# Attention block on one core: ring copies ahead of the store of the denominators, and four smaller moves

## What is computed

```
h = _layernorm(x, ln1_g, ln1_b)
x = _attention(h, h, sa_wq, sa_wk, sa_wv, sa_wo, sa_bo) + x
h = _layernorm(x, ln2_g, ln2_b)
x = _attention(h, cond_emb, ca_wq, ca_wk, ca_wv, ca_wo, ca_bo) + x
h = _layernorm(x, ln3_g, ln3_b)
p = h @ ff_w1 + ff_b1
a, gate = (p[..., :D_FF], p[..., D_FF:])
h = a * jax.nn.gelu(gate, approximate=False) @ ff_w2 + ff_b2
return h + x
```

## Time and profile before

| | us |
|---|---|
| median of three runs | 1690.47 |
| lowest and highest | 1689.78, 1691.63 |
| profiled execution, its time | 1689.77 |
| profiled execution, its span | 1687.9 |
| PE busy | 1676.3 |
| DVE busy | 1396.7 |
| ACT busy | 1249.1 |
| POOL busy | 1082.0 |

### The profile page before, as it was taken

One profiled execution on the slowest core, in us unless ns is written; L12 is line 12 of the kernel. 1 busy time (PEld: TensorE's weight loads), 2 busy tenths in 40 slices (PEclk: granted clock), 3 DMA queues, 4 the chain that ended last, 5 costly groups with the idle time before them and its releaser, 6 DMA issues.

```text
span 1687.9 us, 39061 instructions
## 1 busy us (share of the span) xinstructions
PE 1676.3 (99%) x11712; PEld 1560.7 (92%) x11712; DVE 1396.7 (83%) x2964; ACT 1249.1 (74%) x3378; POOL 1082.0 (64%) x1804
## 2 busy tenths in 40 slices
PE   8999999999999999999999999999999999999999
PEld 8999999999999999999999999999999998888888
DVE  7888788888888888888888888888888987656665
ACT  7788788888888888888888888888888886232221
POOL 7776577777766667687777777777777564231111
PEclk9999999999999999999999999999999999999999
DMA  7776677777776667887787878787776776112110
GB/s 209 187 181 161 171 197 198 205 202 212 198 181 158 158 166 201 233 221 181 192 211 188 210 198 209 195 207 187 191 188 173 196 209 169 51 50 76 62 39 26
DMA packets 301137, 288.91 MB, mean 171 GB/s; under 512 B 103424, under 2 KB 252032, under 8 KB 300928
## 3 DMA queue, kind: packets, MB, share of 16 engines
q1 hardware_dynamic: 246848, 272.76, 61.9%
q10 hardware_dynamic: 54080, 13.65, 3.6%
HBM read 82.98 MB, written 37.49 MB: 71 GB/s over the span
## 4 chain that ended last, share of the span: by engine, by line
PE 96%; DVE 1%; DMA 1%; SPq 0%; issue 0%; ACT 0%; ACTq 0%; DVEq 0%
PE QKB L564 17%; PE PVB L648 14%; PE PTB L577 13%; PE WOP L630 11%; PE VB L499 9%; PE S L466 7%; PE S L467 7%; PE S L1330 5%; PE PTB L1330 5%; PE QKB L546 3%; PE QKB L1352 3%; PE VB L1352 3%; PE QKB L1295 0%; DMA XR<-in_x_dram 0%; DMA HF<-rows 0%
## 5 line engine op out<-in xcount | busy, mean ns | idle before, releaser
L791 ACT ACTIVATE PT<-S,NM 128x256 f32<-128x256 f32 x1024 | 471.9, 473 | 139.2 <-DVE NM L995 138.5
L897 DVE TENSOR_TENSOR PL<-PTB,PH 128x512 fp32r<-128x512 f32 x512 | 350.8, 686 | 123.8 <-ACT PH L819 122.3
L1189 POOL TENSOR_TENSOR ON<-ON,RB 128x256 f32<-128x256 f32 x256 | 188.5, 736 | 272.2 <-DVE ON L1014 247.8
L995 DVE TENSOR_REDUCE NM<-S 128x2 f32<-128x512 f32 x512 | 327.4, 681 | 1.2 <-PE S L467 1.1
L819 ACT ACTIVATE PH<-PTB 128x1024 fp32r<-128x1024 f32 x256 | 264.0, 1031 | 72.0 <-PE PTB L577 71.1
L577 PE MATMUL PTB<-IDN,PT 128*128 128x128 f32 x2048 | 265.5, 272 | 0.6 <-DVE PL L897 0.5
L466 PE MATMUL S<-RX 128*128 128x256 f32 x1012 | 254.0, 283 | 2.1 <-DMA RX<-QKS 2.1
L467 PE MATMUL S<-RX 128*128 128x256 f32 x1012 | 253.7, 283 | 0.0
L564 PE MATMUL QKB<-HT,WQ 128*128 128x512 f32 x936 | 242.0, 394 | 0.2
L630 PEld LDWEIGHTS WOP<-WO,OT 128*128 128x128 f32 x1536 | 217.5, 190 | 19.7
L577 PEld LDWEIGHTS PTB<-IDN,PT 128*128 128x128 f32 x2048 | 229.6, 140 | 1.3 <-DVE PL L897 0.8
(11 more groups left out here) (162 smaller groups left out, 2921.8 us busy)
## 6 DMA issues: line engine op xcount, KB each, us to landing
RX<-QKS SPq DMA_DIRECT2D x506, 192.0 KB, 2.9
RX<-QKS SPq DMA_DIRECT2D x506, 128.0 KB, 2.8
RB<-denominators SPq DMA_DIRECT2D x512, 64.0 KB, 2.7
out_dram<-XR SPq DMA_DIRECT2D x32, 256.0 KB, 3.4
weights_qk<-SPL SPq DMA_DIRECT2D x32, 256.0 KB, 3.4
WQ<-weights_qk SPq DMA_DIRECT2D x32, 256.0 KB, 3.3
rows<-XN SPq DMA_DIRECT2D x23, 256.0 KB, 2.7
rows<-HF SPq DMA_DIRECT2D x22, 256.0 KB, 2.7
```

Source lines behind the costliest of these rows:

```text
L791: last = e.activation(PT[:, c % 2, j * S:(j + 1) * S], S1[:, i, qt * S:(qt + 1) * S], ACT.Exp, bias=NM[:, j:j + 1], accum_out=DEN[:, c % 2 ...
L897: e.tensor_tensor(PL[:, cols], PTB[:, i, :], PH[:, s % 2, cols].bitcast(F32), ALU.subtract).then_inc(a.dve_pl, 1)
L995: e.tensor_reduce(NM[:, i * TT:(i + 1) * TT], S1[:, i, :].rearrange("p (t s) -> p t s", t=TT), AX.X, ALU.max, negate=True).then_inc(a.dve_ ...
```

## The change

SP: from slot 8 on (`PAIRS <= c`) the four ring copies stand ahead of the store of the denominators; in slots 1 to 7 the store stays ahead. The last two quarters of WQ for the feed-forward part are loaded from ACT's queue (`act_load_last`), one chunk at the end of each slot from 248 to 255. PE: behind the last slot the gates of unit 5 stand ahead of the second product of unit 1. In the first slots: DVE normalizes both tiles of sequence 1 in slot 1 instead of one in slot 0 and one in slot 1; the second low part of P of pair 1 is made in slot 2 rather than slot 3; ACT and POOL split weight piece 11 in slot 3 rather than slot 2; POOL splits three pieces of WO at the end of slot 1 and the fourth at the start of slot 2, rather than two in each.

```diff
@@ dve_slot
             if c == 0:
                 dve_weights(e, 5)
-                e.wait_ge(a.pe_h, 2)
-                dve_normalize(e, sl, a, 1, (near(1),), (0,))
-                dve_split_qk(e, 2)
...
-            if c > 2 and sl.has(c - 2) and c < ATT - 1:
+            if c > 3 and sl.has(c - 2) and c < ATT - 1:
                 dve_p_low(e, c - 2, 1)
...
                 e.tensor_copy(VF[:, v // 2 % 2, v % 2, :], VB[:, 0:S]).then_inc(a.dve_vf, 1)
+            if c == 0:
+                dve_split_qk(e, 2)
             if c == 1:
-                dve_normalize(e, sl, a, 1, (near(1),), (1,))
+                e.wait_ge(a.pe_h, 2)
+                dve_normalize(e, sl, a, 1, (near(1),))
...
-                if c == 1 or c >= ATT - 2:
+                if c in (1, 2) or c >= ATT - 2:
                     dve_p_low(e, c - 1, 1)
@@ pool_weights, pool_slot
-            if 1 <= c <= 2:
-                pool_split_wo(e, 0, 0, 2 * c - 2)
-                pool_split_wo(e, 0, 0, 2 * c - 1)
+            if c == 1:
+                pool_split_wo(e, 0, 0, 0)
+                pool_split_wo(e, 0, 0, 1)
+                pool_split_wo(e, 0, 0, 2)
...
+            if c == 2:
+                pool_split_wo(e, 0, 0, 3)
@@ act_attention_slot
+        def act_load_last(e, c):
+
+            quarter, chunk = divmod(c - LAST, 4)
+            if 0 <= quarter < 2:
+                if chunk == 0:
+                    for done in d_ws:
+                        e.wait_ge(done, 16 * QTR * NCH)
+                    e.wait_ge(a.pe_qk, nth_alone(ATT - QUAD + 2 * quarter + 1) + 1)
+                    e.wait_ge(d_wq[quarter], 16 * 4 * (QTR // 2 + 1))
+                e.dma_start(WQ[:, 2 + quarter, chunk, :, :].bitcast(F32), WSQ[1, :, 2 + quarter, chunk, :, :]) \
+                    .then_inc(d_wq[quarter], 16)
+
         def act_attention_slot(e, sl):
             act_slot(e, sl)
-            if -AHEAD <= sl.c < 3:
-                act_weights(e, *((4,), (5,), (6, 7), (8,), (9, 10), (11,))[sl.c + AHEAD])
+            act_load_last(e, sl.c)
+            if -AHEAD <= sl.c < 2 or sl.c == 3:
+                act_weights(e, *((4,), (5,), (6, 7), (8,), (9, 10), (), (11,))[sl.c + AHEAD])
@@ pool_attention_slot
-            if 0 <= sl.c < 3:
-                pool_low(e, *((8,), (10,), (11,))[sl.c])
+            if 0 <= sl.c < 2 or sl.c == 3:
+                pool_low(e, (8, 10, 10, 11)[sl.c])
@@ block.sync
-                if 1 <= c <= ATT:
+                if 1 <= c < PAIRS:
                     save_den(c - 1)
                 if 0 <= c - 1 + AHEAD < ATT and c - 1 >= -AHEAD:
                     k = c - 1 + AHEAD
                     if k >= DIRECT:
                         copy_ring(e, k)
+                if PAIRS <= c <= ATT:
+                    save_den(c - 1)
@@ block.tensor
             pe_second(e, 0)
-            pe_second(e, 1)
             pe_outputs(e, ATT - 2)
             pe_gates(e, EARLY + 1)
+            pe_second(e, 1)
             pe_second(e, 2)
```

More of the change, by code:

```diff
@@ L1711, in fill_weights @@
                 for phase, first in ((0, SLOTS), (1, ATT)):
[L1712 to L1721, removed]
+                    for quarter in range(QTR - 2 * phase):
+                        j = first - 2 * PAIRS + 4 * quarter + 3
+                        freed = nth_joint(j) + 1
                         for chunk in range(4):
-                            if c == at + turns[chunk]:
+                            if c == j - LEAD + 2 + chunk:
                                 if chunk == 0:
@@ L1727, in fill_weights @@
                                     if quarter > 1:
-                                        e.wait_ge(d_wq[quarter % 2], 16 * 4 * (QTR // 2 * phase + quarter // 2))
+                                        e.wait_ge(d_wq[quarter % 2], 16 * 4)
                                 load_quarter(phase, quarter, chunk)
```

## The result

| | before | after |
|---|---|---|
| median, us | 1690.12 | 1947.87 |
| lowest and highest, us | 1688.44, 1691.63 | 1947.42, 1951.58 |
| span of the profiled execution, us | 1687.9 | 1949.8 |

Four runs of each give a ratio of 1.1532, 95% interval 1.1518 to 1.1545: the change costs 258 us. The prediction was 1876 us in a range of 1770 to 1990, so the direction and the range held, and the time came out 72 us above the sum.

A forecast was written before the change was run, and what follows sets the result against it. PE, busy 1676.3 of 1687.9 us, bounds the kernel before; after the change SP's 6.19 us cycle exceeds PE's 5.48. Sum: 1689.8 + 189 - 2.2 - 0.5 - 0.5 = 1876 us, range 1770 to 1990 for 8 in 10.

The forecast's parts named there:

- Part 1: SP's queue from slot 8: the read waits for the denominators' store issued behind the ring copies, so SP sets pace; +189 us.
- L = 2.4: Time in us from the issue of the denominators' store on SP to its landing, in its new place behind four ring copies.
- rival B: The store's flight is that of a loaded machine, 3.25 us in every slot: 2084 us; chance of above 2.9 us: 0.1.
- The cycle around L: SP's slot outside the store's flight: reads 1.20, four ring copies 2.53, satisfied waits 0.06, together 3.79 us; with the flight 6.19.
- Row stores: In 30 slots a store of normalized rows stands between reads and ring on SP, 0.66 us each, not hidden: 20 us.
- The lead of SP: SP's ring copies at first run ahead of PE's need, which takes 4.5 us off the loss.
- Part 2: PE after the last slot: unit 5's gates ahead of unit 1's second product remove a stall, -2.2 us.
- Part 3: Eight last 256 KB refills move from SP's to ScalarE's queue, one a slot from slot 248: 0 to -1 us.
- Part 4: Moves in the first slots remove PE waits of 0.6 and 0.5 us: -0.5 us, between -1.1 and +1.
- A: The store's flight is under 1.69 us, so SP keeps PE's pace and the gains stay: 1686 us; chance 0.05.
- C: Pauses of PE, some 0.7 us in each slot, bring its clock down; chance 0.02.
- D: Something other than SP, VectorE behind its wait for the store, makes the cycle longer than SP's own; chance 0.03.

The follow-up runs named there:

- half-swapped kernel: The changed kernel with the new order of ring copies and store only from slot 128 on, store first in slots 1 to 127: 1836.45 us, ratio 1.0870.

## Why the prediction was right in its mechanism and 72 us short

**Part 1, the mechanism: right.** The loss is the swap's (1.1537 alone, 0.9985 without it), it goes when the read doesn't wait (0.9994), and it doesn't go when VectorE doesn't (1.1578). "SP's waits for the landing should number about 245 and sum to some 400 us": 250 and 367.9.

**L = 2.4: right.** Over the 212 slots from 8 to 251 in which no rows are stored, read off SP's timeline after, the time from the store's issue to the next read is 2.39 in the mean and 2.34 in the median. That was the value of the first of the three places in the earlier trace rows, and the 3.25 of the second, rival B's, is rare: the longest here is 3.57.

**The cycle around L: mis-sized.** In the same 212 slots the reads to the ring take 1.31 and the ring to the store 2.72, together 4.03 where 3.79 was set down (with L, 6.41 instead of 6.19). An ordinary slot takes 1.23 + 2.64 in the median, 0.08 more than was set down. The rest, the larger part, is in single issues: one that takes 0.6 as a rule now and then takes 0.9 to 2.0. One such slot, whose pair of reads takes 2.30 where the next slot's takes 1.13, so that 7.43 us lie between them:

```profile
92.44 2.30 SPq L1661 DMA_DIRECT2D RB<-denominators  x2
...
99.87 1.13 SPq L1661 DMA_DIRECT2D RB<-denominators  x2
```

45 of the 212 slots are over 6.6 us. The kernel before has nearly as many slow issues (46 single ones over 0.9 us or pairs of reads over 1.5, against 51 here), but there SP had slack to absorb them, and the rows chosen for the sum were undisturbed ones; a queue with no slack pays each. 212 x 0.22 = 47 us.

**Row stores: mis-sized.** 20 us were set down for 30 of them, 0.66 each. There are 32 in these slots, and a slot with one takes 7.60 in the mean: 1.19 more than the others: 0.64 for the issue, 0.20 in the ring's issues and 0.33 in L, which is 2.72 there, by rounded means. 32 x (7.60 - 6.19 - 0.66) = 24 us. The two terms give 71 us, which is what the stretch took beyond the forecast: 1602.5 against 245 x 6.19 + 20 - 4.5 = 1532 us. The lead of SP at the start was not read off by itself. The few us that are left of the difference are the 3.1 us of slots 253 to 255 and the gain of Part 2, of which next to nothing shows in the changed kernel.

**The Trainium skill's rule on completion.** The floor that the prediction worked out from the Trainium skill (DMA: Bandwidth & Descriptors, Queues, rings and completion order), a completion that lands only behind the earlier writes of its engine, was 2.15 us for L, with +128 us for the change. The measured 2.34 to 2.39 lies above the floor and the loss is twice that sum, so as a floor for the usual slot it holds (it was reckoned from a median landing; the shortest single L is 1.99). That the copies ahead set L isn't shown: L doesn't grow from two to four of them (2.39, 2.40, 2.36 where SP stood idle ahead of the read).

**Part 2: right about the stall, half wrong about the gain.** What the step left out is that with the outputs POOL's next work comes earlier too. "Nothing else is late" was read from durations that VectorE only has while POOL rests. In the changed kernel itself, PE waits 0.28 and 0.54 us at the change-over, and from slot 255 to the end only 0.1 us is gained.

The Trainium skill (SBUF — State Buffer, Who interferes with whom) has a rule for this: VectorE instructions with two SBUF inputs, or in a mode that uses both of its ports, contend with GpSimd for a port pair, and the second to come waits. The rows above agree in that both engines' instructions get longer (0.43 to 0.85, 0.69 to 1.11, and 2.82 to 4.35 for four); they don't show which instruction blocked which. Put beside the earlier trace rows, the rule would have been a reason to set the gain lower than 2.2.

**Part 3: not told apart from nothing.** 0 to -1 us were set down, and 1.0005 (0.9996 to 1.0013) is -0.7 to +2.2 us. The wait at 1407 went, but it is absent in an execution with the refills still on SP too, and a wait of 0.59 us for RX stands one slot earlier with gates and refills both moved. How many slow issues come together decides it as well; what the refills add isn't shown.

**Part 4: nothing measurable.** The waits of 0.6 and 0.5 us have gone, and 1.0001 (0.9992 to 1.0010) is -1.4 to +1.7 us. The time in these slots scatters by more than the waits are worth: the same first slots have a wait for RX in slot 4 of 0.41 us in the changed kernel and of 2.06 in the one without the swap.

**The rivals.** A, a store that lands in under 1.69 us, is out by its 2.34. B, 3.25 in every slot, is out. C, the clock: "TensorE's clock stays" was wrong. It was granted at 0.992 in the mean, and at 0.979 without VectorE's wait, where it had been 0.999 to 1.000, and it fell to the lower level at or shortly behind pauses of PE. As a cause of the loss C is out all the same: it is at most 0.8% of PE's busy time, 14 us, and SP, which sets the pace, waited for PE's scores once, 0.3 us. D is out by its own experiment. PE's share came out at 92% and not 90%: its busy time rose by 116.5 us for the same matmuls, which the forecast had not counted on. The durations of single matmuls, which overlap, sum to 53 us more, 47 of them in a mean of 303 ns instead of 283 at L466 and about 417 instead of 394 at L564, both of which now often begin behind a pause; how the rest comes about isn't shown. The ends of matmuls are modelled, so the distance between slots is the better measure.

## What to carry to other kernels

Where a DMA waits on its queue for another one to land, it holds all that stands behind it, so the queue needs other work between the two, or the waiting one an older store to read. Before work is moved ahead of a store that is read back, add the queue's cycle up, issue times, flight and all, and set it against the slot of the bounding engine; as long as it fits, waits on that queue cost next to nothing (131 of them, at 0.4%, here), and beyond it each microsecond counts in every slot. Sum such a cycle from the mean over many slots, since a queue without slack pays every slow issue, and take a wait by name for a lead only: when VectorE's wait was removed, PE's merely took another name. A wait that goes in one profile proves little where a second execution without the edit lacks it too. Where a step starts another engine's work earlier, read the durations of both when they run side by side.

## What the runs showed of the hardware

- A DMA issue on SP takes 0.5 to 0.65 us as a rule, but 0.9 to 2.0 in 28 of the 1268 ring copies and stores of the changed kernel (24 in the kernel before), in self and cross attention alike (2.30 instead of 1.13 for a pair, above). What causes it isn't known.
- The store of the denominators, 16 KB to DRAM, is back 2.34 us after its issue in the median (1.99 to 3.57), 0.33 later in the mean behind a row store, and not later behind four ring copies than behind two.
- VectorE and POOL slow each other: 0.75, 0.43 and 0.69 us for one unit's three VectorE instructions became 1.22, 0.85 and 1.11 beside POOL's additions, and these went from 2.82 to 4.35 for four.
- TensorE's clock fell to the lower level, 0.50 of 2.4 GHz, at the end of a single pause of 2.07 us (at 120.4 us of the changed kernel; PE had been busy 8.57 of the 10.40 us before) and was back at 1.00 from 124 us. It did so nine times in that kernel's slots, each time at the end of or within 2 us behind a pause of 1.5 to 2.1 us, while other pauses as long, one of 2.4 us among them, left it at 1.00. Seen over a longer stretch this is easily missed: 0.98 from 1400 to 1500 us of the half-swapped kernel, 0.992 over the whole span.
